# Every queue order, the product order and the bank table of a fused cross-attention and gated feed-forward kernel made anew

## What is computed

```python
query = ctx @ Wq.T + bq;  key = ctx @ Wk.T + bk            # (4, 512, 128), ctx is (4, 512, 256)
attention = softmax(query @ key.T, axis=-1)                # (4, 512, 512)
x = x + layernorm(x) @ attention.T
# _mx_dequant: blocks of 32 along the last dimension, scale = max|block| / 448, value = scale * fp8_e4m3(v / scale)
gate = mx_dequant(y) @ mx_dequant(gate_w).T                # y = layernorm(x), 2048 rows x 512 -> 2048
up   = mx_dequant(y) @ mx_dequant(up_w).T
h    = silu(gate) * up
out  = x + mx_dequant(h) @ mx_dequant(down_w).T            # 2048 -> 512
```

## Time and profile before

| | us |
|---|---|
| runs of the kernel before | 608.98, 609.17, 626.26 (median 609.17) |
| the profiled execution's own time | 610.21 |
| its span, first to last instruction | 608.4 |
| TensorE busy | 596.0 |
| VectorE busy | 484.3 |
| ScalarE busy | 316.6 |
| GpSimd busy | 54.4 |

### The profile page before, as it was taken

How to read it: one execution, slowest core, us unless ns; L and a number is a source line. 1 busy time by engine, 2 the same in 40 slices (tenths; PEclk the granted TensorE clock), 3 DMA queues, 4 the chain that set the end, 5 groups by cost and what they waited for, 6 DMA issues and landing times.

```text
span 608.4 us, 7111 instructions
## 1 busy us (share of the span) xinstructions
PE 596.0 (98%) x2619; PEld 274.1 (45%) x2619; DVE 484.3 (80%) x455; ACT 316.6 (52%) x466; POOL 54.4 (9%) x60
## 2 busy tenths in 40 slices
PE   8998999999999899999999999999999999999998
PEld 3444444444444344444444444444444444444446
DVE  4999879997998998879848598857499699575850
ACT  3999999955444425355735436554031522432441
POOL 0020101310200301001000111010000000000010
PEclk9998999999999999999999999999999999999999
DMA  8968789979677408957786788956432105755393
GB/s 319 392 142 247 234 177 295 229 176 287 136 218 170 112 2 258 219 132 178 193 144 129 160 201 222 172 121 122 86 67 40 17 1 86 106 102 87 70 164 62
DMA packets 148212, 95.43 MB, mean 157 GB/s; under 512 B 134353, under 2 KB 134737, under 8 KB 142801
## 3 DMA queue, kind: packets, MB, share of 16 engines
q1 hardware_dynamic: 142704, 66.92, 46.4%
q0 software_dynamic: 5472, 28.05, 20.1%
HBM read 26.81 MB, written 10.49 MB: 61 GB/s over the span
## 4 chain that ended last, share of the span: by engine, by line
PE 63%; DVE 11%; DMA 10%; ACT 8%; issue 7%; SPq 1%; DVEq 0%; ACTq 0%; POOLq 0%
PE bank L759 26%; PE bank L771 17%; PE bank L774 9%; PE bank L743 5%; DMA W<-hT 3%; PE bank L720 2%; DMA h<-hT 2%; PE bank L728 2%; ACT mag L958 2%; DMA gu_lo<-hT 1%; PE bank L789 1%; DVE h L1680 1%; DVE h L1692 1%; DVE h L1496 1%; DVE hscale L1675 1%
## 5 line engine op out<-in xcount | busy, mean ns | idle before, releaser
L759 PE MATMUL bank<-gu_hi,xT 128*128 128x512 f16 x1024 | 245.1, 379 | 3.9 <-ACT silu L1126 3.8
L759 PEld LDWEIGHTS bank<-gu_hi,xT 128*128 128x128 f16 x1024 | 99.4, 98 | 127.0 <-issue 6.1
L759 PE MATMUL bank<-gu_lo,xT 128*128 128x512 f16 x512 | 131.4, 379 | 0.0
L771 PE MATMUL bank<-dn,hT 128*128 128x512 f16 x480 | 106.1, 379 | 1.2 <-ACT silu L1126 1.2
L1126 ACT ACTIVATE silu<-bank,unscale 128x512 f32<-128x512 f32 x64 | 43.0, 679 | 75.3 <-PE bank L759 34.7
L759 PEld LDWEIGHTS bank<-gu_lo,xT 128*128 128x128 f16 x512 | 50.1, 98 | 60.4
L1663 DVE SCALAR_TENSOR_TENSOR h<-bank,unscale,silu 128x512 f32<-128x512 f32 x64 | 47.1, 747 | 34.4 <-ACT silu L1126 19.4
L771 PEld LDWEIGHTS bank<-dn,hT 128*128 128x128 f16 x480 | 46.9, 98 | 58.1 <-ACT silu L1126 1.7
L1496 DVE SCALAR_TENSOR_TENSOR h<-mag,h 128x2048 f32<-128x2048 bf16 x18 | 41.2, 2289 | 32.0 <-ACT mag L958 32.0
L743 PE MATMUL bank<-dn,h 128*128 128x512 f32 x128 | 57.8, 607 | 1.9 <-ACT dn L1043 1.9
L958 ACT ACTIVATE mag<-h 128x2048 bf16<-128x2048 f32 x18 | 34.3, 1905 | 40.0 <-DVE h L1680 30.5
(11 more groups left out here) (134 smaller groups left out, 569.9 us busy)
## 6 DMA issues: line engine op xcount, KB each, us to landing
W<-hT POOLq DMA_DIRECT2D x12, 1024.0 KB, 6.0
W<-in_units SPq DMA_DIRECT2D x11, 1024.0 KB, 5.8
h<-W POOLq DMA_DIRECT2D x7, 1024.0 KB, 5.9
h<-in_xcols SPq DMA_DIRECT2D x4, 1024.0 KB, 11.1
out_y<-y POOLq DMA_DIRECT2D x12, 256.0 KB, 4.5
h<-in_xrows SPq DMA_DIRECT2D x2, 1024.0 KB, 12.6
h<-hT POOLq DMA_DIRECT2D x2, 1024.0 KB, 6.2
out_y<-h SPq DMA_DIRECT2D x2, 1024.0 KB, 5.1
```

The costliest lines, as they stand in the source:

```text
L759: last = pe.matmul(bank[:, :], xT[:, b % 2, part, k, :], w[:, c, g, j * 512:(j + 1) * 512], start=(j == 0 and not low), stop=(j == HT - 1 ...
L771: pe.matmul(bank[:, :], hT[:, r % 2, 0, k, :], dn[:, w, k, :], start=(k == 0 and w == 0), stop=False)
```

## The change

All five lists, `products` and `bank_uses` are replaced; `rounds`, the helpers, the buffers and the arithmetic are the same. The number of calls is the same but for some of the bare waits between them. In the kernel after, every line below the tables stands 4 lines further down (L1126 is L1130). Of the tables a line each:

```diff
-    products = [(3, 0), (1, 0), (2, 0), (0, 0), (1, 1), (3, 1), (0, 1), (2, 1), (6, 0), (4, 0), (5, 1), (6, 1),
+    products = [(1, 0), (2, 0), (3, 0), (0, 0), (3, 1), (1, 1), (2, 1), (5, 1), (6, 1), (0, 1), (4, 1), (6, 0),
...
-        ("p0.0 p1.0 p1.1 e1.0 t0.0 t0.3 a0.0 e2.3 a1.1 a2.2 a3.2 u0.1 u6.2 g5.2 u7.1 u8.0 u9.1 g10.0 g10.2"
+        ("p0.0 e0.1 p1.1 t0.0 e1.2 t2.1 e3.2 a2.3 u1.0 g3.0 a3.3 g6.1 u4.1 g2.2 g5.2 g4.2 u0.2 u3.3 u4.3"
...
```

SyncE's list at its start:

```diff
+            load_consts()
             load_slice(0)
             load_ctx(0)
-            load_consts()
             load_half(0)
             load_rest(0)
+            load_rows(0)
             load_ctx(1)
             load_unit(1)
-            load_rows(0)
-            load_rows(2)
             load_ctx(2)
+            load_rows(1)
...
```

TensorE's list at its start:

```diff
             project(0, 0)
             project(0, 1)
-            project(1, 0)
             energies(0, 0)
             energies(0, 1)
-            project(1, 1)
             energies(0, 2)
             energies(0, 3)
-            energies(1, 0)
...
+            project(1, 0)
+            project(1, 1)
+            project(2, 0)
+            project(2, 1)
+            turn_probs(0, 0)
+            energies(1, 0)
```

More of the change, by code:

```diff
@@ L848, in _ @@
             attend(1, 2)
+            attend(1, 3)
             turn_probs(2, 0)
-            attend(1, 3)
+            energies(3, 1)
             turn_probs(2, 1)
@@ L854, in _ @@
             energies(3, 2)
+            attend(2, 0)
             energies(3, 3)
-            attend(2, 0)
             attend(2, 1)
@@ L1240, in _ @@
             weigh(2, 2)
-            unit_hi(2)
+            exponential(3, 0)
             weigh(2, 3)
@@ L1246, in _ @@
             take_probs(2, 3)
-            row_variances(1, 1)
+            row_means(2, 0)
+            unit_hi(2)
             rows_hi(0)
-            row_means(2, 0)
+            row_means(2, 1)
             exponential(3, 1)
-            row_means(2, 1)
+            row_variances(2, 0)
             exponential(3, 2)
-            unit_lo(2)
+            row_variances(2, 1)
+            rows_lo(0)
             exponential(3, 3)
-            rows_lo(0)
             weigh(3, 0)
             weigh(3, 1)
-            row_variances(2, 0)
@@ L1276, in _ @@
-            take_probs(3, 3)
-            rows_magnitude(1)
-            row_means(3, 1)
+            weigh(3, 3)
+            take_probs(3, 0)
+            center_by_scalar(1, 0)
+            take_probs(3, 1)
+            unit_magnitude(3)
+            attended_variances(1, 0)
+            center_by_scalar(1, 1)
+            take_probs(3, 2)
+            silu_of(1, 0)
+            unit_rescale(3)
+            unit_lo(2)
+            silu_of(2, 0)
+            row_means(3, 0)
+            take_probs(3, 3)
@@ L1279, in _ @@
+            unit_hi(3)
+            attended_variances(1, 1)
+            rows_magnitude(1)
+            center_by_scalar(2, 0)
+            unit_lo(3)
+            row_means(3, 1)
+            silu_of(3, 0)
             row_variances(3, 0)
-            unit_lo(3)
-            row_variances(3, 1)
+            silu_of(0, 0)
             unit_magnitude(4)
             rows_hi(1)
+            row_variances(3, 1)
+            rows_lo(1)
             unit_rescale(4)
-            silu_of(0, 0)
-            silu_of(1, 1)
@@ L1287, in _ @@
-            unit_hi(4)
-            rows_lo(1)
-            unit_magnitude(5)
-            center_by_scalar(2, 0)
-            unit_lo(4)
+            unit_hi(4)
+            silu_of(3, 1)
+            attended_variances(2, 0)
+            unit_magnitude(5)
+            unit_lo(4)
+            silu_of(1, 1)
+            silu_of(2, 1)
             unit_rescale(5)
-            silu_of(3, 1)
+            silu_of(5, 1)
+            attended_variances(2, 1)
+            unit_rescale(6)
+            unit_hi(5)
@@ L1307, in _ @@
+            unit_lo(6)
+            silu_of(4, 0)
+            silu_of(5, 0)
+            silu_of(2, 2)
             unit_rescale(7)
-            silu_of(5, 0)
-            unit_magnitude(7)
-            unit_lo(6)
             rows_magnitude(2)
+            silu_of(1, 2)
+            unit_hi(7)
+            silu_of(5, 2)
+            unit_magnitude(8)
+            unit_rescale(8)
             silu_of(6, 2)
+            unit_lo(7)
+            silu_of(4, 2)
+            silu_of(0, 2)
+            unit_rescale(9)
```

894 lines of the change are left out of this document (432 added, 462 removed), and 10 rows, old and new, of the table products.

## The result

The kernel after took 621.71 us (median of 4 runs, 620.48 to 623.68) against 609.11 for the kernel before in the same comparison: ratio 1.020, 95% interval 1.018 to 1.022. That is slower by 12.6 us, 9.2 us beyond the end of the predicted range. (One of the four runs before, of 626.26 us, fell in a slower state of the chip and is not in the ratio.) The profiled execution took 621.94 us and its span is 620.1 us, 11.7 more than before. In the kernel after every line stands 4 lower, so L986 is `unit_lo`, L1130 `silu_of`, L763 `product`, L747 `attend`.

The account below looks back on a forecast made before the run. TensorE, busy 596.0 of 608.4 us, was taken as the bound. Span 608.4 + 1.5 - 1.8 + 1.0 - 3.3 + 0.5 = 606.3; 608.1 with surroundings, 607.1 on the median's scale, plus 0.5: 607.6 us, range 602.0 to 612.5.

Parts of the forecast that it names:

- the floor: Whole kernel: 599.6 us would be left if all avoidable TensorE losses in attention and products went.
- The start: First loads reordered, constants first and context third: TensorE begins at the same time, no cost.
- The attention: Stage before the products: scattered small waits replace the old ones, +1.5 us, bounds -2.5 and +5.
- Rival B: Front of the attention: late rows of sequence 0 delay ScalarE and slow the clock, 611.7 us; chance 0.18.
- Products up to 200 us: The wait at 199.5 us goes, -1.8 us; waits of 0.3 and 0.7 us replace it, +1.0.
- The transfer at a constant 6.0 us: Length assumed in the hand-made time order for GpSimd's accumulating transfers, taken from the earlier trace.
- The rule of the Trainium skill: SyncE loads stretch GpSimd's accumulating transfers; margins under 1 us beside them would fall, sum nearer 609 us.
- Products from 200 us on: Stretch from 200 us: old losses of 3.3 us go, some thin margins fail, -3.3 + 0.5 us.
- the last row tiles: Rows 12 to 15: three landings in sequence still leave 3 us in hand; cost 0, up to 2 us.
- the end: Five down products instead of four between the last product and the last down; parts come in time, 0 us.
- A, the waits only move: Products: ScalarE still stands behind GpSimd's transfers, about 5.1 us lost again elsewhere; 610.7 us at full price, chance 0.22.
- B's sign: A clock of 0.50 within the first 90 us would show the slower front.

Follow-up runs that it names:

- two copies: Kernel before, with two needless 1 MB copies issued by SyncE beside unit 7's accumulating transfer: 620.02 us, ratio 1.016.
- the moved store: Kernel after, with SyncE's store of rows 2 moved from ahead of unit 6's accumulating transfer to behind that unit's first transpose: 617.80 us, one run.
- the last of these versions: Kernel after with the old order of first loads, silus ahead of lower parts, and three more moves on ScalarE's list: 610.80 us, ratio 1.0012.
- one copy: Kernel before, with one needless 1 MB copy issued by SyncE beside unit 7's accumulating transfer: 615.58 us, ratio 1.008.
- silus ahead: Kernel after, with silus on ScalarE moved ahead of the lower parts of units 3, 4 and 6, one right behind unit 3's: 617.55 us, ratio 1.010.

## Why the prediction was wrong, point by point

**What bounds the kernel, and the floor.** Right: only order was at stake, and where its losses go, the kernel with five silus moved comes to 606.7 us.

**The start.** Wrong. The step said that TensorE begins at the same time, since constants and context change places. It took the last of the three loads to land at the same time in any order. Before, the last were the constants, issued at 1.65 us and landed at 6.15; after, it is the context, issued at 1.64 us and landed 5.9 us later, at 7.6, with the two loads of 321 and 128 KB ahead of it. The bytes are the same; why the context needs 1.4 us more as the last one stays open. The projections began 1.46 us later, at 7.69 against 6.23, and the slow clock made the first eight matmuls 1.5 us longer (5.15 us against 3.60 to 3.85 at full clock), none of which was in the sum.

**The attention.** The size of +2 us (of which I took 1.5) was met by +2.1, but by luck, since the terms are others: 3.0 us of start and clock, which I had not, less the 3.5 us of the wait of 1.87 us and its clock fall, which went as said, and some 1.4 us of small waits in their place. About 1 us is left over that no row resolves. No wait between 20 us and the products is longer than 0.49 us: the first turn waits that long in place of 0.6, and those of 0.9 and of 1.6 us (first turn of sequence 3) are not there. Rival B's rows of sequence 0 are not the cause either: half a `row_means` begins on ScalarE at 16.26 us, right behind the exponential ahead of it. The rows were issued at 3.10 us and took 10.3, so they landed at 13.4 us, past the 13.3 that I had called decisive; but the late start had moved the exponential to 15.58 us, so nothing waited for them.

**Products up to 200 us.** This is the step that failed: "-1.8 + 1.0". The wait at 199.5 us did go. In its place stand 1.85 + 2.36 + 3.41 = 7.62 us and 6.2 us of clock, where the 0.3 and 0.7 us stood. Two figures in it were too small.
- *The transfer at a constant 6.0 us.* It stood in the sum for every accumulating transfer, out of the earlier trace rows. In the chain after they take 8.38, 7.02, 9.16, 5.77 and 10.49 us. The lists after put a load or a store of 1 MB beside all of these but the one of 5.77 us. The two copies (5.98, 10.61, 13.35 us) and the moved store (10.49 to 6.8) show that this is the cause. With 10.49 - 5.98 = 4.5 us less, nothing is left of the wait of 3.41 us at `unit_lo(6)`, which I had seen as 0.7. The wait of 1.85 us behind `unit_lo(3)` was not in my sum at all: its transfer took 7.02 us, only 1 us more than I had, so there the order of ScalarE's list is the larger part.
- *No clock in the sum.* Every new wait was priced at its length. Four of them brought 1.2 GHz for several us.

The rule of the Trainium skill ("DMA: Bandwidth & Descriptors", "Queues, rings and completion order"), that an engine takes its queues in turn, pointed the right way: the trace agrees that the transfer of GpSimd is stretched by what SyncE issued (7.0 to 10.5 us in place of 6.0), but not in the manner of it (last section). I drew from it that margins of under 1 us would fall, 609 us. The stretch is 1 to 4.5 us per transfer in the kernel after, and 7.4 beside two copies, so that margins of 4 us fall too. The row that I took for agreement, 8.5 us for the transfer dn<-dn, was the wrong one: it was issued at 230.34 us, 1.5 us behind another transfer of GpSimd's own, and not in the stretches of the earlier trace rows. The kernel before has a fitting row, the transfer issued at 169.44 with a load of a unit from 167.40 on ahead of it, which took 6.8 us.

**Products from 200 us on, the last row tiles, the end.** Right. The waits of 1.51 and 1.23 us are gone, rows 12 to 15 came in time, and this part gained 2.3 us of idle (3.3 us lost before to 430 us, 1.0 after; I had 0.5). The last stage is as it was.

**The rivals.** A, the waits only move, describes what happened by its mechanism: in-order ScalarE behind GpSimd's transfers, with silus releasing 7.6 us of waits beyond 100 us, where I had set the mark at 3 us. But its price was what the products had lost before, 5.1 us, and nothing in it let a moved wait be longer than the old, nor the clock fall with it. The clock was in B alone, and there for the attention. No rival joined the two, so the chance for slower by over 2% was 0.03. B's sign, a clock of 0.50 in the first 90 us, is there too, but at 8 to 10 us, behind the late context, which is not B's mechanism; the waits that I had foretold at sequence 3's first turn did not come. A stall of 13 us in one place was what I looked for. In its place the three waits in the products (7.6 us) with their clock (6.2) and the late start (1.5) with its clock (1.5) make 16.8 us, the old losses that went (1.87, 1.53, 1.51, 1.23 and 1.6 of clock) pay 7.7, and the 2.6 us up to 11.7 are new waits of under 1 us and what the rows do not resolve.

**How the difference divides.** From the ratios: three places of silus 1.03% (6.3 us, clock and longer transfers in it), the order of three loads 0.6% (3.8 us), three further silus and variances 0.3% (1.6 us), 11.7 us of 12.4. The rest, 0.1%, is not resolved from nothing. The intervals leave each of the first two open by some 0.4% and the third by 0.25%, so the sizes are rough and the third is barely there. These are what the edits give in this order; they overlap with the store's 4 us (of one run), which is another way to remove one of the same waits.

**What stays open.** Which of the products' new places makes rows 1 late at 139.67 us in the last of these versions was not tried. Nor was a longer distance between all loads and all accumulating transfers. No list was put back as a whole, so what each of the five does by itself is not known. Why the clock falls behind one wait and not behind another is not settled (below).

## What to carry to other kernels

Before a list is written anew, look for in-order pairs in which a short instruction that releases TensorE stands behind one that waits for a DMA, and put it ahead: five silus moved so made the better of the two kernels 0.6% faster, and in the other the same kind of move took back 1.0 and 0.3 of the 2.0%. Price a transfer not by one row, but by what else is issued within some 10 us of it; give it a range (here 5.8 to 10.5 us) and count a wait as long as its late end. And let each new wait of about 2 us or more carry a chance of a clock fall worth 1.5 to 3 us, since that can double its price.

## What was not expected of the hardware

**The stretch of an accumulating transfer.** 1 MB by GpSimd's queue: 5.98 us in a place with little beside it, 10.61 beside one copy of 1 MB, 13.35 beside two. In 188.7 to 194.7 us of the kernel before and 179.0 to 189.5 of the kernel after, the two transfers ran in these windows:

```profile
188.70:194.70 6.00, 6.00 (x29) 2.74 (x28) 5.92 (x6) 0.00 (x0) 0.87 (x1) 1.00 0.68 178
```

```profile
179.00:189.50 10.50, 10.32 (x48) 4.50 (x46) 9.21 (x6) 1.04 (x2) 1.05 (x1) 1.00 0.93 287
```

A DMA share of 0.68 and 178 GB/s against 0.93 and 287: the engines were not waiting, they moved other bytes.

The packets in the traces show more, and most of the stretch stands ahead of the transfer's own first packet:

| transfer | beside it | us from issue to its first packet | first to last packet | issue to landing |
|---|---|---|---|---|
| before, 188.73 | nothing | 1.4 | 4.2 | 5.98 |
| before, 169.44 | a load | 2.3 | 4.1 | 6.8 |
| after, 162.20 | nothing | 1.4 | 4.0 | 5.77 |
| after, 142.07 | a store | 3.7 | 5.2 | 9.16 |
| after, 179.02 | a load and a store | 4.8 | 5.2 | 10.49 |
| store moved, 179.77 | a load | 2.1 | 4.4 | 6.8 |
| one copy, 187.92 | 16 packets of 64 KB | 4.7 | 5.6 | 10.61 |
| two copies, 187.57 | 32 packets of 64 KB | 7.3 | 5.8 | 13.35 |

With nothing beside it the first packet starts 1.4 us after the issue. Beside two copies all 32 packets of the copies start ahead of it, the second 16 of them from 191.0 us on, and in the kernel after at 179.02 all 128 packets of the load and 251 of the store. Only behind its first packet do its packets of 8 KB alternate with the store's of 2 KB. Strict turns from the moment of issue would look otherwise; why the first packet is late is not shown. What to ask of a list is thus how much SyncE has issued when the transfer starts. The copies are not an exact image of the loads (packets of 8 KB) and stores (2 KB), so their 4.6 and 2.7 us are not prices for those.

**A small load ahead of the first one that counts.** With two loads of 449 KB together ahead of the context's 512 KB its way from issue to landing is 5.9 us (6.8 in the kernel before with the new order of loads); with 128 KB alone ahead of it, it was 3.5 us.

**The clock falls irregularly.** It fell to 0.50 behind waits of 1.85, 2.36 and 3.41 us (after), 1.87 (before), 2.80 (silus ahead), 2.93, 3.40, 4.06, 4.13, 5.27, 6.14 and 8.89, and behind 2.66 us at the start. It stayed at 1.00 behind 1.77 and 3.71 us (old order of loads, all else as after), 1.52, 1.63, 1.84, 1.94 and 3.06 us, and behind the same wait of 1.86 us in the attention of the kernel before, once three loads had another order or a copy was added 130 us later. Length alone does not decide it. The kernel before itself shows that this is partly chance. It ran 45 times as the reference of the experiments, on two chips; in 23 of these runs the clock over the span was 0.997, in 22 it was 0.999 or 1.0, and the mean times are (us):

| comparison | clock 0.997 | clock 0.999 or 1.0 | difference |
|---|---|---|---|
| first (11 runs) | 611.58 | 609.51 | 2.1 |
| second (21 runs) | 610.83 | 609.43 | 1.4 |
| third (13 runs) | 611.46 | 609.99 | 1.5 |

The runs at 0.997 are 1.4 to 2.1 us longer, near the 1.6 us read from the earlier trace rows for one fall, and such a fall comes in half of the runs with not one instruction changed. The page "TensorE: Matmul & The Clock Gate" of the Trainium skill, "What's actually happening", ties the clock to how busy the engine has been of late; the rows agree in that every fall stands behind a wait or begins in it, and do not tell which wait brings one.
